# Gated LoRA and low-rank FFN on one core: gh of pairs 1 to 6 transposed by VectorE and by SBUF transfers

## Chip, core and metric

One Trainium2 chip, one core of it. The metric is the device time of the kernel in microseconds (us). Three runs of the kernel before gave 154.99, 155.07 and 155.89 us; the median is 155.07 us.

## What is computed

Cut to what matters, the reference is (x is 2048 x 1024, seen as 32 x 64 rows of 1024; all in float32):

```python
base   = x @ W.T                                   # W 1024 x 1024
logits = x @ Wr.T + 5.0 * one_hot(language_id)     # 8 experts
gates  = softmax over the top 2 logits, 0 for the other experts
h      = x @ A[e].T                                # 8 experts x rank 16
lora   = sum over e, r of h[e, r] * gates[e] * B[e, :, r]
c      = base + 2.0 * lora
out    = x + c @ (U * S @ V.T).T                   # rank 256
```

## The kernel before, in words

The host lays the data out; the kernel never forms base. Since c is only used through V, it first makes P = W.T V (1024 x 256) and BV = 2 B.T V (128 x 256), and then for every row of x: z = x P + gh BV, out = x + z (U S).T, where gh (128 values a row, 8 experts x 16) is h times its gate. All products are float32 split in a high and a low part (x = hi + lo), three matmuls for one: `triple` (L333 to L336) issues hi x hi, lo x hi, hi x lo.

x has 16 tiles of 128 rows. Tiles 2p and 2p+1 are pair p, p from 0 to 7. Names by stage:

- `project(t)` (L379): 8 triples on tile t into bank pj[t % 2], 264 columns: 128 of h, 8 logits, 128 of z (the first half of P's columns). For even t from 2 on, after its fifth triple, `mix(t/2 - 1)` is put in.
- `half_t(p)` (L396): the other half of z, made already transposed (8 triples of 256 columns, both tiles of the pair) in bank zt. After its sixth triple two TensorE transposes (L405) add the first half of z, which ScalarE has copied to z_sb (`copy_z`).
- `transpose_gh(p)` (L413): two TensorE transposes of gh into bank gt (L418). ScalarE casts them to ghT_hi (L624), VectorE subtracts for ghT_lo (L777).
- `mix(p)` (L421): two triples that add gh BV to zt. After it ScalarE and VectorE split zt into hi and lo (`split_za`), and sums of its quarters (`copy_x22`, `sums`, `split_zb`) feed a product of seven terms instead of eight.
- `first_part(p)` (products 1, 6, 7, 5, 2) and `second_part(p)` (products 4, 3), each product one triple of 512 columns into one of four banks fin. VectorE adds them up (`up`) and adds them to x (`xb1`, `xa0`, `xb0`, `xa1`), POOL does three additions more (`sides`, L296).

The order is written out by hand, one instruction list for each engine; semaphores join them. The steady order on PE, for p from 2: project(2p) with mix(p-1), first_part(p-2), project(2p+1), second_part(p-2), half_t(p), transpose_gh(p). VectorE's gates of tile t (`gates_top`, `gates_apply`, ten small operations with the exponential on ScalarE between them) end in gh. SP issues all loads and stores in the steady part: for every p two xt tiles, two x tiles, then the two stores of pair p-2. POOL also makes xT_lo of every tile (L281, 2.4 us), the second one of a pair only when gh of tile 2p+1 is written. Before the pairs stands a stage in which W arrives and P is built; POOL's xT_lo of tile 0 falls into it.

Of the kernel before, what the change touches and what calls it, by code (L numbers as in the profile page):

```python
# [16 lines left out]
def adaln_ffn(nc, xt, x, ids, VW, W, AW, B, U, S, out):  # L17
    P = 128
# [27 lines left out]
    with ExitStack() as ctx:  # L46
# [52 lines left out]
        w_flat = w_raw[:, :, :].rearrange("p c n -> p (c n)")  # L99
        b_raw = w_flat[:, 0:OC * ER].rearrange("p (c n) -> p c n", c=OC)  # L100
# [12 lines left out]
        gt_both = gt[:, 0:2 * P]  # L113
        bv_ps = gt[:, RANK:2 * RANK]
        zt_v = zt[:, :].rearrange("p (m t n) -> p m t n", m=MC, t=2)
# [41 lines left out]
        gt_done = sem("gt_done")  # L157
        gt_hi = sem("gt_hi")
# [22 lines left out]
        LAG = 4  # L181
        PRODS = 7
# [12 lines left out]
        def _(sp):  # L195
# [74 lines left out]
        def _(pool):  # L270
# [12 lines left out]

            def make_tsum(j):
# [20 lines left out]
            split_x(0)  # L305
# [26 lines left out]
        def _(pe):  # L332
# [46 lines left out]
            def project(t):  # L379
# [5 lines left out]
                for k in range(DC):  # L385
# [6 lines left out]
                    if t >= 2 and t % 2 == 0 and k == MH:  # L392
# [3 lines left out]
            def half_t(p):  # L396
                r = (2 * p) % XTR
                dst = zt_v[:, 1, :, :]
                for k in range(DC):
                    last = triple(dst, proj_hi[:, k, TCOLS:COLS], proj_lo[:, k, TCOLS:COLS],  # L400
                                  xT_hi[:, r:r + 2, k, :], xT_lo[:, r:r + 2, k, :], k == 0, False, shared=True)
                    if k == MH + 1:
                        pe.wait_ge(z_copied, 2 * p + 2)
                        for t in range(2):
                            nc.tensor.matmul(zt_v[:, 0, t, :], z_sb[:, t, :], ident[:, :], start=False, stop=False,  # L405
# [7 lines left out]
            def transpose_gh(p):  # L413
                pe.wait_ge(gh_done, 2 * p + 2)
                if p >= 1:
                    pe.wait_ge(gt_lo, p)
                for t in range(2):
                    last = nc.tensor.transpose(gt[:, t * P:(t + 1) * P], gh[:, t, :], ident[:, :])  # L418
                last.then_inc(gt_done, 1)

            def mix(p):  # L421
# [3 lines left out]
                for m in range(MC):  # L425
                    cols = slice(m * P, (m + 1) * P)
                    last = triple(zt[:, 2 * m * P:2 * (m + 1) * P], bv_hi[:, cols], bv_lo[:, cols],
# [94 lines left out]
            for p in range(1, PAIRS):  # L522
# [8 lines left out]
                transpose_gh(p)  # L531
# [24 lines left out]
        def _(act):  # L556
# [41 lines left out]
            def split_za(p):  # L598
                act.wait_ge(zt_done, p + 1)
                zh_free(p)  # L600
                nc.scalar.copy(zh[:, p % 2, 0:MC, :], zt_v[:, :, 0, :]).then_inc(za_hi, 1)

            def split_zb_plain(p):
                act.wait_ge(za_lo, p + 1)
                nc.scalar.copy(zh[:, p % 2, MC:2 * MC, :], zt_v[:, :, 1, :]).then_inc(zb_hi, 1)

            def copy_x22(p):
                if p >= 1:
                    act.wait_ge(zb_lo, p)
                nc.scalar.copy(zs[:, 0, :], zt_v[:, 1, 1, :]).then_inc(x22_copied, 1)  # L610
# [11 lines left out]
            def split_gh(p):  # L622
                act.wait_ge(gt_done, p + 1)
                nc.scalar.copy(ghT_hi[:, :], gt_both).then_inc(gt_hi, 1)  # L624
# [9 lines left out]
            def pair(p):  # L634
                if p < PAIRS - 1:
                    split_x(2 * p + 2)
                split_za(p - 1)
                copy_x22(p - 1)
                copy_u(p - 2)
                copy_z(2 * p)  # L640
                exp_top(2 * p)
                split_zb(p - 1)
                if p < PAIRS - 1:
                    split_x(2 * p + 3)
                copy_z(2 * p + 1)
                exp_top(2 * p + 1)
                split_gh(p)
# [49 lines left out]
            exp_top(3)  # L697
            split_x(5)
            split_gh(1)
# [8 lines left out]
        def _(dve):  # L708
# [66 lines left out]
            def split_gh(p):  # L775
                dve.wait_ge(gt_hi, p + 1)
                nc.vector.tensor_sub(ghT_lo[:, :], gt_both, ghT_hi[:, :].bitcast(F32)).then_inc(gt_lo, 1)  # L777
# [6 lines left out]
            def split_za(p):  # L784
# [3 lines left out]
                nc.vector.tensor_sub(zl[:, p % 2, 0:MC, :], zt_v[:, :, 0, :],  # L788
                                     zh[:, p % 2, 0:MC, :].bitcast(F32)).then_inc(za_lo, 1)

            def split_zb_plain(p):
                dve.wait_ge(zb_hi, p + 1)
                nc.vector.tensor_sub(zl[:, p % 2, MC:2 * MC, :], zt_v[:, :, 1, :],
                                     zh[:, p % 2, MC:2 * MC, :].bitcast(F32)).then_inc(zb_lo, 1)

            def sums(p):
                n = 4 * p
                nc.vector.tensor_add(zs[:, 1, :], zt_v[:, 0, 1, :], zs[:, 0, :]).then_inc(sums_done, 1)
                dve.wait_ge(sums_done, n + 1)
                nc.vector.tensor_sub(zs[:, 2, :], zs[:, 1, :], zt_v[:, 0, 0, :]).then_inc(sums_done, 1)  # L800
                dve.wait_ge(sums_done, n + 2)
                nc.vector.tensor_sub(zs[:, 3, :], zs[:, 0, :], zs[:, 2, :]).then_inc(sums_done, 1)
                nc.vector.tensor_sub(zs[:, 4, :], zt_v[:, 1, 0, :], zs[:, 2, :]).then_inc(sums_done, 1)
# [40 lines left out]

            def pair_2():
# [126 lines left out]
```

## Time and profile before

| | |
|---|---|
| median of three runs | 155.07 us |
| profiled execution, its own time | 155.31 us |
| its span | 153.5 us |
| ScalarE's cast to ghT_hi (L624), mean of 8 | 372 ns |
| ScalarE's cast of zs (L614), mean of 7 | 710 ns |
| ScalarE's copy to z_sb (L628), mean of 16 | 266 ns |
| POOL's addition in `sides` (L296), mean of 21 | 1298 ns |
| load of an xt tile, median from issue to landing | 7.4 us |
| POOL's xT_lo of a tile (L281), mean of 16 | 2404 ns |

The span is that of the profiled execution on the chip; a time in it is read from the span's start. Matmuls overlap: a record lasts longer than the distance to the next one, so what a matmul costs PE is read from the chain of waits, which gives each piece the time until the next one starts. "Idle before" names who released an engine that had stood still.

### The profile page before, as it was taken

Reading aid. Unit: us, or ns where it says so; the run is one execution under the profiler, and the core shown is the slowest. Engines: PE = TensorE matmul, PEld = TensorE weight load, DVE = VectorE, ACT = ScalarE, POOL = GpSimd, SP = SyncE. Lnnn points to the kernel's source line nnn. Section 1 sums busy time; section 2 is a strip of 40 time slices with the busy share of each in tenths; the row PEclk is TensorE's granted clock in tenths of the full one; section 3 lists DMA queues with packets and bytes.
Section 4 is the critical chain, followed back from the end, with each engine's and each line's share of the span. In section 5 each row is a group of like instructions: output and inputs, shape, how many; then the busy total and the mean of one; then the engine's idle time right before and its main releaser. Section 6 shows DMA issues by size and latency. Waiting matters only on the chain.

```text
span 153.5 us, 2910 instructions
## 1 busy us (share of the span) xinstructions
PE 148.2 (97%) x1056; PEld 139.3 (91%) x1056; DVE 106.6 (69%) x297; ACT 63.5 (41%) x141; POOL 71.2 (46%) x56
## 2 busy tenths in 40 slices
PE   7999999999999999899999999999999999999991
PEld 5899989999999988898999899989999998998880
DVE  0776896769578999948674875587559746785951
ACT  3576877884636423346204611361334104013000
POOL 2000233992660666582866196627664640631800
PEclk9999999999999999999999999999999999999999
DMA  5999999999104040069509912990482068006184
GB/s 169 364 386 414 399 409 411 410 406 411 70 4 137 0 137 0 4 255 352 212 19 361 384 62 97 351 367 11 179 265 107 0 260 273 19 0 273 68 334 144
DMA packets 10669, 32.72 MB, mean 213 GB/s; under 512 B 1440, under 2 KB 1952, under 8 KB 10528
## 3 DMA queue, kind: packets, MB, share of 16 engines
q1 hardware_dynamic: 10368, 31.96, 55.4%
q10 hardware_dynamic: 288, 0.59, 1.0%
q8 instruction: 8, 0.13, 0.3%
q14 instruction: 5, 0.04, 0.1%
HBM read 24.16 MB, written 8.39 MB: 212 GB/s over the span
## 4 chain that ended last, share of the span: by engine, by line
PE 80%; DMA 6%; DVE 5%; SPq 4%; issue 2%; DVEq 1%; ACT 0%
PE fin L334 10%; PE pj L335 9%; PE pj L334 9%; PE fin L336 9%; PE fin L335 9%; PE pj L336 9%; PE zt L336 6%; PE zt L334 6%; PE zt L335 6%; DMA xt_raw<-in_xt 6%; SPq L197 2%; DVE w_lo L713 2%; SPq L220 1%; PE gt L418 1%; PE zt L405 1%
## 5 line engine op out<-in xcount | busy, mean ns | idle before, releaser
L281 POOL TENSOR_TENSOR xT_lo<-xt_raw,xT_hi 128x1024 fp32r<-128x1024 f32 x16 | 38.4, 2404 | 40.9 <-ACT xT_hi L582 21.2
L296 POOL TENSOR_TENSOR x_all<-x_all,vw_raw 128x512 f32<-128x512 f32 x21 | 26.6, 1298 | 28.2 <-DVE vw_raw L818 26.3
L334 PE MATMUL pj<-proj_hi,xT_hi 128*128 128x264 f32 x128 | 36.9, 288 | 0.0
L335 PE MATMUL pj<-proj_lo,xT_hi 128*128 128x264 f32 x128 | 36.3, 284 | 0.0
L336 PE MATMUL pj<-proj_hi,xT_lo 128*128 128x264 f32 x128 | 36.2, 283 | 0.0
L334 PE MATMUL fin<-v_hi,w_hi 128*128 128x256 f32 (+1 forms) x88 | 28.1, 320 | 0.2 <-DVE w_lo L713 0.2
L335 PE MATMUL fin<-v_lo,w_hi 128*128 128x256 f32 (+1 forms) x88 | 27.9, 317 | 0.0
L336 PE MATMUL fin<-v_hi,w_lo 128*128 128x256 f32 (+1 forms) x88 | 27.9, 317 | 0.0
L335 PEld LDWEIGHTS pj<-proj_lo,xT_hi 128*128 128x128 f32 x128 | 24.1, 189 | 0.2
L334 PEld LDWEIGHTS pj<-proj_hi,xT_hi 128*128 128x128 f32 x128 | 24.1, 188 | 0.2
L336 PEld LDWEIGHTS pj<-proj_hi,xT_lo 128*128 128x128 f32 x128 | 24.0, 188 | 0.0
L334 PE MATMUL zt<-xT_hi,proj_hi 128*128 128x256 f32 x64 | 18.6, 291 | 0.0
L336 PE MATMUL zt<-xT_hi,proj_lo 128*128 128x256 f32 x64 | 18.0, 281 | 0.0
L335 PE MATMUL zt<-xT_lo,proj_hi 128*128 128x256 f32 x64 | 17.9, 280 | 0.0
L824 DVE TENSOR_TENSOR x_all<-fin,x_all 128x512 f32<-128x512 f32 x28 | 17.9, 682 | 0.0
L334 PEld LDWEIGHTS fin<-v_hi,w_hi 128*128 128x128 f32 x88 | 16.6, 189 | 1.4 <-DVE w_lo L713 0.4
L336 PEld LDWEIGHTS fin<-v_hi,w_lo 128*128 128x128 f32 x88 | 16.6, 189 | 1.2
L335 PEld LDWEIGHTS fin<-v_lo,w_hi 128*128 128x128 f32 x88 | 16.6, 189 | 0.8
L582 ACT CAST xT_hi<-xt_raw 128x1024 fp32r<-128x1024 f32 x16 | 16.8, 1049 | 1.0 <-DMA xt_raw<-in_xt 1.0
L628 ACT COPY z_sb<-pj 128x128 f32<-128x128 f32 x16 | 4.3, 266 | 22.8 <-DVE logit L745 22.8
L334 PE MATMUL fin<-us_hi,w_hi 128*128 128x512 f32 (+1 forms) x31 | 11.9, 383 | 0.8 <-DVE x_all L824 0.8
L335 PEld LDWEIGHTS zt<-xT_lo,proj_hi 128*128 128x128 f32 x64 | 12.0, 188 | 0.3
(93 smaller groups left out, 272.6 us busy)
## 6 DMA issues: line engine op xcount, KB each, us to landing
xt_raw<-in_xt SPq DMA_DIRECT2D x16, 512.0 KB, 7.4
x_all<-in_x SPq DMA_DIRECT2D x16, 512.0 KB, 6.5
out<-x_all SPq DMA_DIRECT2D x13, 512.0 KB, 3.1
vw_raw<-in_VW SPq DMA_DIRECT2D x6, 384.0 KB, 8.0
w_raw<-in_W SPq DMA_DIRECT2D x8, 256.0 KB, 7.4
out<-x_all SPq DMA_DIRECT2D x5, 256.0 KB, 2.0
w_raw<-in_U SPq DMA_DIRECT2D x1, 1024.0 KB, 6.9
aw_raw<-in_AW SPq DMA_DIRECT2D x1, 544.0 KB, 8.1
```

Of the source, the lines that this page charges most:

```text
L197: sp.dma_start(w_raw[:, k, :], W[k, :, :]).then_inc(w_load[k], 16)
L220: sp.dma_start(vw_raw[:, k, :], VW[k, :, :]).then_inc(vw_load[k], 16)
L281: nc.gpsimd.tensor_sub(xT_lo[:, t % XTR, :, :], xt_raw[:, t % XTR, :, :], xT_hi[:, t % XTR, :, :].bitcast(F32)).then_inc(xt_lo, 1)
L296: nc.gpsimd.tensor_add(x_all[:, t % XR, cols], x_all[:, t % XR, cols], ups[:, j, :]).then_inc(side_add, 1)
L334: nc.tensor.matmul(dst, l_hi, r_hi, start=first, stop=False, skip_group_check=shared)
L335: nc.tensor.matmul(dst, l_hi, r_lo, start=False, stop=False, skip_group_check=shared)
L336: return nc.tensor.matmul(dst, l_lo, r_hi, start=False, stop=last, skip_group_check=shared)
L405: nc.tensor.matmul(zt_v[:, 0, t, :], z_sb[:, t, :], ident[:, :], start=False, stop=False, is_transpose=True, skip_group_check=True)
L582: nc.scalar.copy(xT_hi[:, t % XTR, :, :], xt_raw[:, t % XTR, :, :]).then_inc(xt_hi, 1)
L628: nc.scalar.copy(z_sb[:, t % 2, :], pj[t % 2][:, Z0:TCOLS]).then_inc(z_copied, 1)
L713: nc.vector.tensor_sub(w_lo[:, i % WRING, :], w_chunk(i), w_hi[:, i % WRING, :].bitcast(F32)).then_inc(w_lo_done, 1)
L824: nc.vector.tensor_add(x_all[:, t % XR, cols], src[:, :], x_all[:, t % XR, cols]).then_inc(fin_read, 1)
```

## The change

VectorE turns gh of pairs 1 to 6 in 32 x 32 blocks from gh into `blk`, each block in its own place (`turn_gh`). The blocks off the diagonal then have to change places: SP issues twelve SBUF-to-SBUF transfers of 32 partitions x 2 tiles x 32 columns from `blk` to `tr` (`move_blocks`), and ScalarE copies the four diagonal blocks (`move_diagonal`). `blk` and `tr` lie in the unused part of w_raw and have two slots each. ScalarE and VectorE make ghT_hi and ghT_lo from `tr` (`split_gh_moved`). Pairs 0 and 7 keep the TensorE transposes; that of pair 7 writes into pj[0].

With it go these moves. mix(p-1) for pairs from 1 on stands in project(2p+1), not in project(2p). zt alternates between two banks, zt and gt, and `zt_free` waits for the pair before the last. VectorE's and ScalarE's order inside a pair is changed, and xT_lo of tile 0 is made in two halves.

```diff
+        blk = w_flat[:, 8 * P:12 * P].rearrange("p (q m n) -> p q m n", q=2, m=2)
+        tr = w_flat[:, 16 * P:20 * P].rearrange("p (q m n) -> p q m n", q=2, m=2)
...
-        zt_v = zt[:, :].rearrange("p (m t n) -> p m t n", m=MC, t=2)
+        zt_bank = [zt, gt]
+        zt_v = [b[:, :].rearrange("p (m t n) -> p m t n", m=MC, t=2) for b in zt_bank]
...
+            def move_blocks(p):
+                sp.wait_ge(blk_done, p)
+                for i in range(SQS):
+                    for j in range(SQS):
+                        if i != j:
+                            sp.dma_start(tr[SQ * j:SQ * (j + 1), p % 2, :, SQ * i:SQ * (i + 1)],
+                                         blk[SQ * i:SQ * (i + 1), p % 2, :, SQ * j:SQ * (j + 1)]).then_inc(tr_load, 16)
...
                     load_x(2 * p + 1)
+                if p < PAIRS - 1:
+                    move_blocks(p)
                 if p >= 2:
                     store_pair(p - 2)
...
-            split_x(0)
+            split_x_half(0, 0)
+            split_x_half(0, 1)
...
-                    if t >= 2 and t % 2 == 0 and k == MH:
+                    if t == 2 and k == MH:
+                        mix(0)
+                    if t >= 5 and t % 2 == 1 and k == MH:
                         mix(t // 2 - 1)
...
             def zt_free(p):
-                pe.wait_ge(za_lo, p)
-                pe.wait_ge(sums_done, 4 * p)
+                if p == 1:
+                    pe.wait_ge(bv_lo_done, 1)
+                if p >= 2:
+                    pe.wait_ge(za_lo, p - 1)
+                    pe.wait_ge(sums_done, 4 * (p - 1))
...
                 half_t(p)
-                transpose_gh(p)
+            transpose_gh(PAIRS - 1)
...
+            def split_gh_moved(p):
+                act.wait_ge(tr_load, MOVES * p)
+                act.wait_ge(tr_diag, SQS * p)
+                nc.scalar.copy(ghT_hi[:, :], tr[:, p % 2, :, :]).then_inc(gt_hi, 1)
+
+            def move_diagonal(p):
+                act.wait_ge(blk_done, p)
+                for i in range(SQS):
+                    rows = slice(SQ * i, SQ * (i + 1))
+                    nc.scalar.copy(tr[rows, p % 2, :, rows], blk[rows, p % 2, :, rows]).then_inc(tr_diag, 1)
...
             def pair(p):
                 if p < PAIRS - 1:
                     split_x(2 * p + 2)
+                copy_u(p - 2)
+                if p == 2:
+                    split_gh_moved(1)
+                copy_z(2 * p)
+                exp_top(2 * p)
+                if p < PAIRS - 1:
+                    split_x(2 * p + 3)
+                if p >= 3:
+                    split_gh_moved(p - 1)
                 split_za(p - 1)
                 copy_x22(p - 1)
-                copy_u(p - 2)
-                copy_z(2 * p)
-                exp_top(2 * p)
                 split_zb(p - 1)
-                if p < PAIRS - 1:
-                    split_x(2 * p + 3)
                 copy_z(2 * p + 1)
                 exp_top(2 * p + 1)
-                split_gh(p)
+                if p < PAIRS - 1:
+                    move_diagonal(p)
+                else:
+                    split_gh(p)
...
+            def turn_gh(p):
+                dve.wait_ge(gh_done, 2 * p + 2)
+                nc.vector.transpose(blk[:, p % 2, :, :], gh[:, :, :]).then_inc(blk_done, 1)
...
             def pair(p):
-                split_zb(p - 2)
-                split_za(p - 1)
-                sums(p - 1)
-                gates_top(2 * p)
-                gates_apply(2 * p)
-                up(p - 2, 1)
-                up(p - 2, 2)
-                xb1(p - 2)
-                xa0(p - 2)
-                gates_top(2 * p + 1)
-                gates_apply(2 * p + 1)
-                xb0(p - 2)
-                xa1(p - 2)
-                if p == PAIRS - 1:
-                    split_zb(p - 1)
-                split_gh(p)
+                gates(2 * p)
+                up(p - 2, 1)
+                up(p - 2, 2)
+                split_gh_moved(p - 1)
+                xb1(p - 2)
+                xa0(p - 2)
+                split_za(p - 1)
+                sums(p - 1)
+                gates(2 * p + 1)
+                if p < PAIRS - 1:
+                    turn_gh(p)
+                    xb0(p - 2)
+                    xa1(p - 2)
+                    split_zb(p - 1)
+                else:
...
+                    split_gh(p)
```

VectorE, pair 4, from the end of its first gates on, before (w_lo is zl and vw_raw is ups, which lie in those tiles; the rows of the second gates are left out):

```order
L770 SCALAR_TENSOR_TENSOR gh<-pj,rsum,gate 128x128
L818 TENSOR_TENSOR vw_raw<-fin,vw_raw 128x512 x2
L824 TENSOR_TENSOR x_all<-fin,x_all 128x512 x2
L745 SCALAR_TENSOR_TENSOR logit<-target,pj 128x8
...
L770 SCALAR_TENSOR_TENSOR gh<-pj,rsum,gate 128x128
L824 TENSOR_TENSOR x_all<-fin,x_all 128x512 x2
L777 TENSOR_TENSOR ghT_lo<-gt,ghT_hi 128x256
L807 TENSOR_TENSOR w_lo<-zs,w_hi 128x640
L788 TENSOR_TENSOR w_lo<-zt,w_hi 128x256
```

The same place with the change (w_raw holds blk and tr):

```order
L819 SCALAR_TENSOR_TENSOR gh<-pj,rsum,gate 128x128
L877 TENSOR_TENSOR vw_raw<-fin,vw_raw 128x512 x2
L831 TENSOR_TENSOR ghT_lo<-w_raw,ghT_hi 128x256
L883 TENSOR_TENSOR x_all<-fin,x_all 128x512 x2
L847 TENSOR_TENSOR w_lo<-gt,w_hi 128x256
L857 TENSOR_TENSOR zs<-gt,zs 128x128
L859 TENSOR_TENSOR zs<-zs,gt 128x128
...
L819 SCALAR_TENSOR_TENSOR gh<-pj,rsum,gate 128x128
L836 STREAM_TRANSPOSE w_raw<-gh 128x256
L883 TENSOR_TENSOR x_all<-fin,x_all 128x512 x2
L866 TENSOR_TENSOR w_lo<-zs,w_hi 128x640
```

ghT_lo now reads `tr` in SBUF and stands between `up` and xb1; the splits of zt (w_lo, zs) come before the second gates, and the block transpose right behind them.

SP with the change, pair 3 (w_raw<-w_raw are the twelve transfers):

```order
L210 DMA xt_raw<-in_xt 128x1024 x2
L215 DMA x_all<-in_x 128x1024 x2
L255 DMA w_raw<-w_raw 32x2x32 x12
L219 DMA out<-x_all 128x1024
L221 DMA out<-x_all 128x1024
```

Twelve issues stand between the loads of a pair and the stores of the pair before the last; before, nothing stood there.

## Rows read from the trace of the kernel before

**Rows 1.** The page: busy us, share of the span, instructions.
```profile
PE 148.2 (97%) x1056; PEld 139.3 (91%) x1056; DVE 106.6 (69%) x297; ACT 63.5 (41%) x141; POOL 71.2 (46%) x56
```

**Rows 2.** Windows: length, busy of PE, PEld, DVE, ACT, POOL, clock, DMA, GB/s.
```profile
50.50:66.20 15.70, 14.86 (x106) 13.66 (x105) 14.02 (x35) 5.24 (x13) 10.28 (x6) 1.00 0.11 34
95.37:109.95 14.58, 14.58 (x105) 13.73 (x105) 9.70 (x33) 5.05 (x13) 8.60 (x6) 1.00 0.59 217
```

**Rows 3.** Chain of waits, pair 5: start us, us, what.
```profile
95.37 0.12 PE pj L334
...
97.18 0.12 PE zt L334
...
98.98 0.23 PE fin L334
...
102.39 0.12 PE pj L334
...
105.29 0.23 PE fin L334
...
106.67 0.12 PE zt L334
...
108.80 0.22 PE zt L405 x2
...
109.73 0.22 PE gt L418 x2
```

**Rows 4.** Timeline of PE, pair 2: start us, us, instruction, idle before.
```profile
60.73 0.39 PE L336 MATMUL fin<-v_hi,w_lo 128*128 128x512 f32 x1
61.95 0.50 PE L334 MATMUL fin<-us_hi,w_hi 128*128 128x512 f32 x1 [0.84 <-DVE x_all L824]
```

**Rows 5.** Timeline while P is built: PE, POOL, VectorE.
```profile
20.81 0.28 PE L336 MATMUL fin<-v_hi,w_lo 128*128 128x256 f32 x1
21.32 0.38 PE L334 MATMUL fin<-v_hi,w_hi 128*128 128x256 f32 x1 [0.22 <-DVE w_lo L713]
...
18.31 2.39 POOL L281 TENSOR_TENSOR xT_lo<-xt_raw,xT_hi 128x1024 fp32r<-128x1024 f32 x1 [16.43 <-ACT xT_hi L582]
...
18.78 2.48 DVE L713 TENSOR_TENSOR w_lo<-w_raw,w_hi 128x512 fp32r<-128x512 f32 x1 [0.59 <-ACT w_hi L567]
```

**Rows 6.** Timeline of SP: issues.
```profile
3.08 0.43 SPq L223 DMA_DIRECT2D ids_i<-in_ids  x1
3.56 0.43 SPq L220 DMA_DIRECT2D vw_raw<-in_VW  x1
...
66.57 2.02 SPq L202 DMA_DIRECT2D xt_raw<-in_xt  x2
```

**Rows 7.** The page, DMA issues: count, KB, median us from issue to landing.
```profile
out<-x_all SPq DMA_DIRECT2D x2, 128.0 KB, 1.9
```

**Rows 8.** Groups by form: busy us, mean ns, idle before.
```profile
L777 DVE TENSOR_TENSOR ghT_lo<-gt,ghT_hi 128x256 fp32r<-128x256 f32 x8 | 3.4, 424 | 10.3 <-ACT ghT_hi L624 10.3
...
L713 DVE TENSOR_TENSOR w_lo<-vw_raw,w_hi 128x512 fp32r<-128x512 f32 x8 | 5.5, 687 | 0.2
```

**Rows 9.** Timeline of VectorE, pair 5.
```profile
99.95 0.15 DVE L745 SCALAR_TENSOR_TENSOR logit<-target,pj 128x8 f32<-128x8 f32 x1
...
101.53 0.35 DVE L770 SCALAR_TENSOR_TENSOR gh<-pj,rsum,gate 128x128 f32<-128x128 f32 x1
101.79 1.51 DVE L818 TENSOR_TENSOR vw_raw<-fin,vw_raw 128x512 f32<-128x512 f32 x2
```

**Rows 10.** Timeline, pair 2: POOL, then VectorE.
```profile
57.50 2.59 POOL L296 TENSOR_TENSOR x_all<-x_all,vw_raw 128x512 f32<-128x512 f32 x2
...
57.31 0.29 DVE L800 TENSOR_TENSOR zs<-zs,zt 128x128 f32<-128x128 f32 x1
57.63 1.30 DVE L802 TENSOR_TENSOR zs<-zs 128x128 f32<-128x128 f32 x1
```

**Rows 11.** The page, DMA queue: packets, MB, share of 16 engines.
```profile
q1 hardware_dynamic: 10368, 31.96, 55.4%
```

More of the change, by code:

```diff
@@ L181, in adaln_ffn @@
         LAG = 4
+        SQ = 32
+        SQS = P // SQ
+        MOVES = 16 * SQS * (SQS - 1)
         PRODS = 7
@@ L282, in split_x, with split_x_half @@
                                      xT_hi[:, t % XTR, :, :].bitcast(F32)).then_inc(xt_lo, 1)
+            def split_x_half(t, h):
+                pool.wait_ge(xt_hi, t + 1)
+                ks = slice(h * MH, (h + 1) * MH)
+                op = nc.gpsimd.tensor_sub(xT_lo[:, t % XTR, ks, :], xt_raw[:, t % XTR, ks, :],
+                                          xT_hi[:, t % XTR, ks, :].bitcast(F32))
+                if h == 1:
+                    op.then_inc(xt_lo, 1)
             def make_tsum(j):
@@ L404, in half_t @@
                         for t in range(2):
-                            nc.tensor.matmul(zt_v[:, 0, t, :], z_sb[:, t, :], ident[:, :], start=False, stop=False,
+                            nc.tensor.matmul(zt_v[p % 2][:, 0, t, :], z_sb[:, t, :], ident[:, :], start=False, stop=False,
                                              is_transpose=True, skip_group_check=True)
@@ L609, in copy_x22 @@
                     act.wait_ge(zb_lo, p)
[L610 removed]
+                nc.scalar.copy(zs[:, 0, :], zt_v[p % 2][:, 1, 1, :]).then_inc(x22_copied, 1)
             def split_zb(p):
@@ L843, in residual_end, with gates @@
                 nc.vector.tensor_add(x_all[:, t % XR, lo:hi], src[:, 0:hi - lo], x_all[:, t % XR, lo:hi]).then_inc(end_read, 1)
+            def gates(t):
+                gates_top(t)
+                gates_apply(t)
             def pair_2():
@@ L847, in pair_2 @@
                 split_us(1)
[L848 removed]
                 up(0, 1)
                 up(0, 2)
+                split_gh_moved(1)
+                xb1(0)
+                gates(4)
+                split_za(1)
                 sums(1)
[L852 to L854 removed]
+                gates(5)
+                turn_gh(2)
                 xa0(0)
[L856 to L857 removed]
                 xb0(0)
                 xa1(0)
[L860 removed]
+                split_zb(1)
             def pair(p):
[L863 removed]
+                gates(2 * p)
[4 more added lines that the diff above has]
+                xa0(p - 2)
                 split_za(p - 1)
                 sums(p - 1)
[L866 to L878 removed]
+                gates(2 * p + 1)
[3 more added lines that the diff above has]
+                    xa1(p - 2)
+                    split_zb(p - 1)
+                else:
+                    split_zb(p - 1)
+                    xb0(p - 2)
+                    xa1(p - 2)
+                    split_gh(p)
             dve.wait_ge(vw_load[0], 16)
@@ L909, in _ @@
             sums(0)
-            gates_top(2)
-            gates_apply(2)
-            gates_top(3)
-            gates_apply(3)
+            gates(2)
+            gates(3)
+            turn_gh(1)
             split_t(1)
-            split_gh(1)
             pair_2()
```

47 lines of the change are left out of this document (23 added, 24 removed).

## The prediction

> **What bounds the kernel now.** I read the busy shares first: TensorE is busy 97% of the span, VectorE 69% [rows 1]. By stretch it is tighter: from the pair that starts at 95.37 us to the next, 14.58 us are 14.58 us of PE; only the pair from 50.50 to 66.20 is longer, 15.70 us with 14.86 busy [rows 2]. The granted clock is 1.00, the 2.4 GHz level, throughout. The chain of waits, read next, is an unbroken row of matmuls in a middle pair, so it gives the schedule of PE [rows 3]. Count from T, the start of project(2p) (95.37): the mix of pair p-1 at T+1.8, first_part at T+3.6, project(2p+1) at T+7.0, second_part at T+9.9, half_t at T+11.3, z's two transposes at T+13.4, gh's two at T+14.36, next pair at T+14.58. So a PE instruction that goes is worth its time there, as long as no other engine comes late. The whole question is whether any does.
>
> **The removed transposes.** The chain gives a pair's two transposes of gh as 0.22 us [rows 3]; the 272 ns of a single record is latency, since the next matmul starts before it ends. Six pairs lose them: 6 x 0.22 = -1.32 us. Pairs 0 and 7 keep theirs. The Trainium skill ("VectorE: DVE Perf Modes", The three transpose paths) gives 390 ns for a 128x128 transpose on TensorE and 311 ns on VectorE, and its rules for authors send a 128x128 transpose to TensorE. By its figure the removal would be an estimate of 6 x 0.78 = -4.7 us; this trace shows 0.22 us for two, and that decides.
>
> **The first tile's split in two halves.** At 18.31 POOL starts xT_lo of tile 0 (2.39 us). VectorE's w_lo at 18.78 has two SBUF inputs and takes 2.48 us, where its sisters take 0.69 [rows 8]: it stands still until POOL is done, and PE starts its next matmul at 21.32 where 20.93 was due by the 0.12 us rhythm [rows 5]. With halves VectorE waits for 1.2 us less, which covers the whole hole: -0.38 us. (Bounds: 0 if the second half gets in ahead of VectorE, -0.4.)
>
> **The new path of gh.** The mix now stands in project(2p+1), so call its start M = T + 7.0 + 5 x 0.36 minus the 0.70 us of mix that leaves project(2p) = T+8.1. The pair is 14.36 us by PE alone. What follows M in today's order: logit starts 2.77 us behind the mix's start (99.95 against 97.18), gh is written at 101.88, so M+4.7 [rows 3, 9]; ScalarE's cast of zs now stands before the exponential of the odd tile and adds some 0.2: gh at M+4.9. Then, none of it in the trace of before:
> - VectorE's block transpose, 128x256. Nearest row: the subtraction of the same size, 0.42 us [rows 8]. I take 0.42; below, half of it; above, twice.
> - Twelve transfers on SP. The issue of 8 KB of ids and the one after it start 0.48 us apart, and both take 0.43, so size is not what counts; with the ring full two took 2.02 us [rows 6]. I take 0.48, because the queue is idle then: the last starts 11 x 0.48 = 5.3 us after the first. Ends: 0.3 us, if fewer rows (32 for 128) make it cheaper, and 1.0 us.
> - Its landing: 1.9 us, as the smallest stores had [rows 7].
> - ScalarE's four diagonal copies (some 0.8 us) lie beside the transfers and cost nothing; without that cover they would be 0.8 us.
> - ScalarE's cast 0.37 us and VectorE's subtraction 0.42 us, as before [rows 8].
>
> Sum with 0.1 us at each hand-over: landed at M + 4.9 + 0.5 + 0.1 + 5.3 + 1.9 = M+12.7, ready for the mix at M+13.6. PE wants it at M+14.36. So the transfers are hidden with 0.75 us to spare, and PE does not wait in a middle pair. The same in T: landed at T+6.4, when VectorE has done gates(2p) and both up adds (about T+6.9).
>
> **A new collision.** ghT_lo was PSUM minus SBUF; of a moved gh it reads two SBUF tiles. Such an operation of VectorE stands still beside POOL: zs at 57.63 took 1.30 us, the zs before it 0.29, up to the end of POOL's first addition; POOL's three additions (1.3 us each) start when up(p-2,1) is done, T+6.2, just ahead of it. In a middle pair VectorE gets in when the first ends, at T+7.5, and is done at T+7.8: 0.3 us to spare. Nothing there, but the cover is thin.
>
> **What queues behind.** On SP the stores of pair p-3 and the loads of xt now come after the twelve issues, 5.6 us later; the xt they bring is cast some 8 us after its issue and lands 7.4 us after it in the median, so it just arrives: nothing. On VectorE the residual adds xb0 and xa1 stand behind the block transpose, 0.42 us; bank_c and bank_d are needed only at T+4.3 of the next pair. Nothing. On POOL the split of tile 2p+3 starts with gh as before.
>
> **Pair 2.** Today PE stands from 60.96 to 61.95 = 0.99 us behind the late VectorE work of this pair [rows 4]. In the new order that add (xb1) is early, but z's copy is late: moves of pair 1 land at about 57.4, ghT_lo is done at 58.2, then xb1 0.7, gates(4) 1.9 plus up to 1.3 behind POOL's additions, za 0.4, sums 1.1, the cast of zs 0.7, copy 0.3: z is there at 63.3 to 64.6, and PE is at z's transposes at 63.7. So the old wait goes and one of 0 to 0.9 comes: -0.99 to 0. I take 0, since dtop and chosen (two SBUF inputs) both fall into POOL's three additions. **Pair 3** then inherits it: gates(5) ends 1.5 us later than in a middle pair, POOL's splits shift with it, the first dtop waits for one of them (2.4 us), up comes at T+7, and ghT_lo runs into the additions and is ready at T+9.2 instead of T+8.1: 0 to +1.2, I take +1.1. After that the middle-pair schedule holds.
>
> **Sum.** -1.32 - 0.38 + 0 + 1.1 = -0.6 us on the profiled execution's 155.31 us (span 153.5): 154.7; it is 0.24 above the median 155.07, so 154.5 us.
>
> **Rivals.**
> 1. *The thin places hold.* No wait in pair 3 and pair 2 between its bounds: -1.7 to -2.7, that is 153.4 to 152.4 us. For it: each collision of pairs 2 and 3 hangs on who starts first within 0.1 us. Against: POOL is busy for most of that pair.
> 2. *The moves come late, slower.* If they land more than 0.75 us later (the transfers' pitch at 0.55 us is enough, or a transpose of 0.84 with a landing of 2.3), ScalarE's cast is done after POOL's second addition has begun, and ghT_lo waits for its end: about +1.1 us in each of five pairs (mixes 2 to 6), one of which the forecast has: 154.5 + 4.4 = 158.9 us. It gets worse if packets, not issues, set the pace: the packets of the main queue took 55.4% of 16 engines x 153.5 us, 131 ns each [rows 11]; a move is 64 packets, four and a closing one on each engine, 0.66 us at that price, 7.9 us for twelve. Ready at M+16.2, the pair would be 16.2 us, +1.8 each: about 163 us. Against: these packets hold 128 B, those 3 KB. The Trainium skill ("DMA: Bandwidth & Descriptors", Measured under Bandwidth) says that transfers under 64 KB are descriptor-dominated and gives 0.68 us for a 4 KB one of 64 packets; by it twelve in a row are an estimate of 8.2 us, and that speaks against the change. No row of before has packets so small, alone.
> 3. *split_zb loses its place.* Behind the residual adds it has two SBUF inputs and meets POOL's split of tile 2p+3, until T+1.2 of the next pair. If POOL then starts tile 2p+4 ahead of it, zb is ready at T+4.4, and PE wants it at T+3.6: +0.8 us in each of three or four pairs, 157 us. For it: POOL's next input is cast at just that time. Against: VectorE has then been waiting, and a waiting VectorE got in between two additions at 58.8 [rows 10].
>
> **Numbers.** Forecast 0.36; rival 1 0.31; rival 2 0.22; rival 3 0.11. I take 1% (1.55 us) as what can be told from no change. Faster by over 1% (under 153.52) is rival 1 and the forecast's edge: 0.33. Slower by over 1% (above 156.62): rival 2 and half of rival 3, 0.27. Within: 0.40. Forecast's own range 153.5 to 155.5. For 8 in 10 the range goes from 152.4, the best sum, to 159.3, past the first step of rival 2; the packet-bound part of it and little else is left out.
>
> **What would show it.** Right: middle pairs of 14.36 us, all PE; SP's twelve issues 0.48 us apart; the last landing at T+6.4; a PE wait before z's transposes in pair 2 and before the mix in project(7). PE waits on ghT_lo in every pair speak for rival 2, on w_lo<-zs for rival 3. A pitch far below 0.4 us or a move landing in under 1.5 us would leave more slack than I give it; a shift of POOL's additions by half a microsecond would change pairs 2 and 3 and make the sum wrong by up to 2 us.

## The result and the profile after

The changed kernel takes 165.95 us (median of 6 runs, 164.61 to 166.85) beside 155.22 us for the kernel before on the same chip: ratio 1.068, 95% interval 1.063 to 1.073. The forecast was 154.5 us in a range of 152.4 to 159.3, so the time lies above all of it. The mechanism that happened is rival 2, the moves that come late; it was given 0.22.

The profiled execution took 164.61 us with a span of 162.8, so 9.3 us more than the 155.31 and 153.5 of before. The page after, busy shares first (they answer [rows 1]), then the queue ([rows 11]), the chain that ended last, and the transfers among the DMA issues:

```profile
PE 148.1 (91%) x1044; PEld 138.3 (85%) x1044; DVE 112.1 (69%) x303; ACT 69.0 (42%) x165; POOL 73.5 (45%) x57
...
q1 hardware_dynamic: 16128, 32.56, 54.6%
...
PE 36%; SPq 25%; DVE 14%; DMA 10%; ACT 8%; issue 4%; DVEq 2%
SPq L255 25%; DMA w_raw<-w_raw 7%; PE fin L361 7%; PE fin L363 7%; PE fin L362 7%; DMA w_raw<-in_W 3%; ACT w_hi L645 2%; PE gt L361 2%; PE pj L361 2%; PE pj L362 2%; PE pj L363 2%; DVE w_raw L836 2%; PE zt L361 2%; DVEq L796 2%; PE gt L363 2%
...
w_raw<-w_raw SPq DMA_DIRECT2D x72, 8.0 KB, 1.8
```

PE is as busy as before in microseconds, and its share of the span is six points lower. A quarter of the critical chain is one line, L255: not the data of the transfers but SP's work of issuing them.

The mixes of the six moved pairs start at 60.29, 77.75, 94.15, 110.15, 126.35 and 141.94 us, so they are 17.5, 16.4, 16.0, 16.2 and 15.6 us apart. Windows of about one such distance each (columns as in [rows 2]; the second is exactly from mix to mix):

```profile
78.50:94.15 15.65, 13.88 (x98) 12.82 (x97) 10.21 (x34) 5.94 (x17) 8.79 (x5) 1.00 0.56 199
94.15:110.15 16.00, 14.63 (x102) 13.57 (x102) 10.98 (x35) 5.94 (x17) 8.93 (x5) 1.00 0.56 196
110.15:126.00 15.85, 14.62 (x101) 13.57 (x101) 10.63 (x34) 5.94 (x17) 8.91 (x5) 1.00 0.58 206
126.00:142.00 16.00, 14.68 (x102) 13.63 (x102) 11.22 (x36) 4.05 (x15) 6.20 (x4) 1.00 0.43 145
```

A pair that took 14.58 us now takes some 16 us, and PE stands in each. What it stands for, PE's waits (us in total, times, longest):

```profile
PE gt L361 <- DVE ghT_lo L831: 5.4, 3, 2.1
PE zt L361 <- DVE ghT_lo L831: 4.3, 3, 2.0
...
PE zt L434 <- ACT z_sb L670: 0.6, 1, 0.6
```

All six mixes of moved pairs wait for ghT_lo, 9.7 us in all. A first matmul behind such a wait takes 0.39 us in the chain where one in a row takes 0.12, 6 x 0.27 = 1.6 more. With 0.6 for z_sb, less the 0.99 of [rows 4] and the 1.32 of the transposes, that is 9.6, against the 9.3 between the two profiled executions.

The chain of waits through one such pair (start us, us, what) shows what holds ghT_lo up:

```profile
94.15 0.39 PE gt L361
...
95.16 0.37 ACT w_hi L632
...
98.90 0.36 DVE gh L819
99.28 0.46 DVE w_raw L836
99.75 0.59 SPq L255
100.39 0.60 SPq L255
...
106.14 1.23 SPq L255
107.42 1.79 DMA w_raw<-w_raw
109.23 0.41 ACT ghT_hi L660
109.67 0.43 DVE ghT_lo L831
110.15 0.39 PE zt L361
```

It is a closed loop of 16.0 us. The mix at 94.15 releases the split of zt; behind that on VectorE and ScalarE come the gates; gh is written at 99.26, turned, moved by twelve issues one behind the other, cast, and only then may the next mix start, at 110.15. PE needs 14.36 us for a pair, so it waits for the loop each time.

The chain names eleven issues; the twelfth starts at 107.42, and the 1.79 us of the DMA piece run from there, from the start of that issue, to the landing. SP's own timeline gives this set and the next (start, us, what):

```profile
99.75 8.26 SPq L255 DMA_DIRECT2D w_raw<-w_raw  x12
115.75 7.63 SPq L255 DMA_DIRECT2D w_raw<-w_raw  x12
```

An issue takes 0.60 us and the next one starts 0.64 us after it. Eleven such steps are 7.0 us; in the set at 99.75 the eleventh issue took 1.23 us, so that the last starts 7.7 us after the first.

### The profile page after: what moved, and what is told of

Read it like the earlier page. It is cut to its first block, busy times and chain, and to the rows that moved or that the text cites. A ratio compares the mean times of both kernels' runs of the same rounds, so it can differ in the third digit from the quotient of the medians.

```text
span 162.8 us, 2987 instructions
## 1 busy us (share of the span) xinstructions
PE 148.1 (91%) x1044; PEld 138.3 (85%) x1044; DVE 112.1 (69%) x303; ACT 69.0 (42%) x165; POOL 73.5 (45%) x57
## 4 chain that ended last, share of the span: by engine, by line
PE 36%; SPq 25%; DVE 14%; DMA 10%; ACT 8%; issue 4%; DVEq 2%
SPq L255 25%; DMA w_raw<-w_raw 7%; PE fin L361 7%; PE fin L363 7%; PE fin L362 7%; DMA w_raw<-in_W 3%; ACT w_hi L645 2%; PE gt L361 2%; PE pj L361 2%; PE pj L362 2%; PE pj L363 2%; DVE w_raw L836 2%; PE zt L361 2%; DVEq L796 2%; PE gt L363 2%
## 5 line engine op out<-in xcount | busy, mean ns | idle before, releaser
L299 POOL TENSOR_TENSOR xT_lo<-xt_raw,xT_hi 128x1024 fp32r<-128x1024 f32 x15 | 37.7, 2522 | 32.6 <-DVE gh L819 18.4
L361 PE MATMUL pj<-proj_hi,xT_hi 128*128 128x264 f32 x128 | 36.4, 284 | 0.0
L831 DVE TENSOR_TENSOR ghT_lo<-w_raw,ghT_hi 128x256 fp32r<-128x256 f32 x6 | 3.2, 538 | 13.6 <-ACT ghT_hi L660 13.6
L363 PE MATMUL fin<-us_hi,w_lo 128*128 128x512 f32 (+1 forms) x31 | 11.7, 377 | 0.0
L362 PE MATMUL fin<-us_lo,w_hi 128*128 128x512 f32 (+1 forms) x31 | 11.7, 376 | 0.0
L877 DVE TENSOR_TENSOR vw_raw<-fin,vw_raw 128x512 f32<-128x512 f32 x14 | 9.6, 687 | 3.0 <-PE fin L363 2.2
L660 ACT CAST ghT_hi<-w_raw 128x256 fp32r<-128x256 f32 x6 | 2.4, 405 | 20.3 <-DMA w_raw<-w_raw 20.3
```

The lines of the kernel that those rows point to most:

```text
L299: nc.gpsimd.tensor_sub(xT_lo[:, t % XTR, :, :], xt_raw[:, t % XTR, :, :], xT_hi[:, t % XTR, :, :].bitcast(F32)).then_inc(xt_lo, 1)
L361: nc.tensor.matmul(dst, l_hi, r_hi, start=first, stop=False, skip_group_check=shared)
L362: nc.tensor.matmul(dst, l_hi, r_lo, start=False, stop=False, skip_group_check=shared)
L363: return nc.tensor.matmul(dst, l_lo, r_hi, start=False, stop=last, skip_group_check=shared)
L877: nc.vector.tensor_add(ups[:, j, :], (bank_b if j == 1 else bank_c)[:, :], ups[:, j - 1, :]).then_inc(fin_read, 1)
```

## Experiments

Times are medians; a ratio is to the kernel before on the same chip, with its 95% interval. The kernel before took 155.11 to 155.22 us beside these experiments, so times of different experiments can be compared to about 0.1 us as far as the chip goes.

### no_moves: the transfers left out

```diff
-                for i in range(SQS):
-                    for j in range(SQS):
-                        if i != j:
-                            sp.dma_start(tr[...], blk[...]).then_inc(tr_load, 16)
...
-                act.wait_ge(tr_load, MOVES * p)
```

> The changed kernel without its 72 transfers: the blocks off the diagonal never change places, so gh of pairs 1 to 6 is wrong; all else is as in the change. Theory A (the issues on SP close a loop from mix to mix that is longer than PE's work): in the change a middle pair is 16.00 us (94.15 to 110.15); without the transfers nothing that is issued stands between the block transpose and the casts, the loop is shorter than PE's 14.36 us and the pair is 14.36. Pairs 3 to 7 give back 5 x 1.6 = 8 us and pair 2 its wait of 2.1: 165.9 - 10 to 12 = 154 to 156 us. Theory B (the new order, the second zt bank or the collisions of VectorE with POOL are what costs): the time stays above 160 us and PE goes on waiting for ghT_lo.

Measured: 154.81 us (154.53 to 155.45), ratio 0.998 (0.997 to 1.000). Everything else of the change, the new order, the block transposes and the diagonal copies, is in this kernel, so the 72 transfers and the wait for them cost 11.1 us in this order (9.8 between the two profiled executions, 164.61 and 154.78). PE's waits in it (timeline, idle before in brackets):

```profile
64.32 0.44 PE L429 MATMUL zt<-ident,z_sb 128*128 128x128 f32 x2 [0.88 <-ACT z_sb L664]
74.25 0.39 PE L356 MATMUL zt<-ghT_hi,bv_hi 128*128 128x256 f32 x1 [0.65 <-DVE ghT_lo L825]
```

These are the two waits that the forecast named, before z's transposes in pair 2 and before the mix in project(7). What it forecast is close to the kernel that one gets when the moves are in time: 154.81 for 154.5. Two errors partly cancel in that: the -0.38 of the first tile's halves did not come (halves_only below), and the wait in project(7) costs 0.65 and the 0.27 of a late first matmul, where 1.1 was entered.

### ten_moves: two transfers fewer in each pair

```diff
-        MOVES = 16 * SQS * (SQS - 1)
+        MOVES = 16 * (SQS * (SQS - 1) - 2)
...
-                        if i != j:
+                        if i != j and (i, j) not in ((0, 1), (1, 0)):
```

> The change with ten transfers a pair instead of twelve (blocks (0,1) and (1,0) are left where they were, so that part of gh is wrong). Theory A, the number of issues times their pitch: two issues of 0.64 us fewer are 1.28 us off every loop, 16.0 to 14.7, still above 14.36. Five loops and the first one: 165.9 - 6 x 1.28 = 158.2 us. Rival A2, the latency of the last landing or a queue that has to drain counts and not the number: under 2 us of gain, 164 to 165 us. Rival B (order and collisions): no change, 165.9 us.

Measured: 157.25 us (156.76 to 157.44), ratio 1.013 (1.011 to 1.015); 8.7 us off for twelve issues in all (7.2 between the profiled executions). Its sets on SP (start, us, count):

```profile
96.15 6.35 SPq L255 DMA_DIRECT2D w_raw<-w_raw  x10
111.67 6.36 SPq L255 DMA_DIRECT2D w_raw<-w_raw  x10
```

Ten take 6.35 us, 0.64 each. From the first set to the sixth it is 75.7 us (50.35 to 126.05), in the change 82.0 (49.93 to 131.95): 1.26 us less a pair in the mean, two issues at 0.64. That is the slope of a loop, one to one, but only in the mean: the five distances are 18.1, 15.4, 16.4, 16.0 and 16.2 us in the change and 16.2, 14.1, 15.5, 15.5 and 14.4 here. Two of the latter are down at PE's own 14.36, and a long issue or a late landing falls into other sets than in the change. PE still waits 3.3 us for ghT_lo, 0.9 at the longest.

### rows256: the same bytes as 32 rows of 256 B, without a third dimension

```diff
-        blk = w_flat[:, 8 * P:12 * P].rearrange("p (q m n) -> p q m n", q=2, m=2)
+        blk = w_flat[:, 8 * P:12 * P].rearrange("p (q j m n) -> p q j m n", q=2, j=4, m=2)
...
-                            sp.dma_start(tr[SQ * j:SQ * (j + 1), p % 2, :, SQ * i:SQ * (i + 1)],
-                                         blk[SQ * i:SQ * (i + 1), p % 2, :, SQ * j:SQ * (j + 1)]).then_inc(tr_load, 16)
+                            sp.dma_start(tr[SQ * j:SQ * (j + 1), p % 2, i, :, :].rearrange("p m n -> p (m n)"),
+                                         blk[SQ * i:SQ * (i + 1), p % 2, j, :, :].rearrange("p m n -> p (m n)")).then_inc(tr_load, 16)
```

The block transpose, the diagonal copies, the cast and the subtraction follow this layout (not shown).

> The same twelve transfers a pair and the same result, with blk and tr laid out so that the 32 columns of both tiles lie side by side: a transfer has 32 rows of 256 bytes instead of 64 of 128. In the change an issue takes 0.60 us, against 0.43 for a full-width load. If the number of rows or the third dimension of the pattern makes the issue dearer (theory A3), it falls to 0.43 and the pitch from 0.64 to 0.48: 11 x 0.16 = 1.8 us off each loop, the middle pair at 14.4, and the whole at 155.5 to 157.5 us. If the issue costs 0.60 because both ends are in SBUF or for another reason that has nothing to do with rows, the time stays at 165 to 166.

Measured: 165.53 us (164.78 to 167.47; without the highest of the four, 165.16), ratio 1.071 (1.064 to 1.078). The issues of the change first, then those of this kernel (ns, least/median/most):

```profile
L255 SPq DMA_DIRECT2D w_raw<-w_raw x72: 586/597/1233, 49.9 to 139.0; - x72
```

```profile
L255 SPq DMA_DIRECT2D w_raw<-w_raw x72: 507/591/1267, 49.7 to 138.6; - x72
```

Half the rows, the same issue, and no gain that can be told from the change. By the queue's count a transfer is 48 packets here (13824 in all, less the 10368 of [rows 11], over 72) and 80 in the change. Neither the packets nor this change of shape set the pace.

### issue_forms: what does the 0.60 us hang on?

Each pair's twelve transfers in another form, to spare columns; order and number as before. One execution, 161.63 us. Its whole time is not the point.

```diff
+                            if p == 1:
+                                sp.dma_start(two[b, :, :], blk[a, d, :, b])...    # 32 x 2 x 128 B, SBUF to SBUF
+                            elif p == 2:
+                                sp.dma_start(flat[b, :], x_v[0, a, 0:64])...      # 32 x 256 B, HBM to SBUF
+                            elif p == 3:
+                                sp.dma_start(two[:, :, :], blk[:, d, :, b])...    # 128 x 2 x 128 B, SBUF to SBUF
+                            elif p == 4:
+                                sp.dma_start(flat[b, :], blk[a, d, 0, 0:64])...   # 32 x 256 B, SBUF to SBUF
+                            elif p == 5:
+                                sp.dma_start(flat[:, :], x_v[0, :, 0:64])...      # 128 x 256 B, HBM to SBUF
+                            elif p == 6:
+                                sp.dma_start(flat[:, :], blk[:, d, 0, 0:64])...   # 128 x 256 B, SBUF to SBUF
```

> Not a time but a measurement of SP's issues: the twelve transfers of every moved pair go to a spare place, in another form for each pair (the exchanged blocks never reach tr, so gh is wrong). Pair 1: as in the change, 32 rows x 2 x 128 B, SBUF to SBUF. Pair 2: 32 rows of 256 B from HBM. Pair 3: 128 rows x 2 x 128 B, SBUF to SBUF. Pair 4: 32 rows of 256 B, SBUF to SBUF. Pair 5: 128 rows of 256 B from HBM. Pair 6: 128 rows of 256 B, SBUF to SBUF. If 0.60 us is the price of both ends in SBUF, pairs 2 and 5 show 0.43 and the others 0.60. If it is the price of 32 rows, pairs 3, 5 and 6 show 0.43. If it is the price of a transfer behind others still in flight, all six show 0.6.

Measured (ns, least/median/most, and when the first and the last started), in the order of the six forms:

```profile
L261 SPq DMA_DIRECT2D w_raw<-w_raw x12: 596/597/756, 49.8 to 57.0; - x12
L263 SPq DMA_DIRECT2D w_raw<-in_x x12: 340/421/427, 67.8 to 72.8; - x12
L265 SPq DMA_DIRECT2D w_raw<-w_raw x12: 593/622/1189, 81.8 to 90.2; - x12
L267 SPq DMA_DIRECT2D w_raw<-w_raw x12: 590/591/1181, 98.7 to 106.2; - x12
L269 SPq DMA_DIRECT2D w_raw<-in_x x12: 328/432/437, 114.6 to 119.7; - x12
L271 SPq DMA_DIRECT2D w_raw<-w_raw x12: 527/601/604, 129.0 to 136.0; - x12
```

All four forms with both ends in SBUF take 0.59 to 0.62 us in the median, with 32 rows or 128, in two dimensions or three. Both forms from HBM take 0.42 to 0.43, one behind the other as well. So of what was varied here the issue's price goes by where the ends lie; larger transfers and other destinations were not in this run. The 0.43 of [rows 6] was the price of a load from HBM.

### split_queue: four of the twelve issued by ScalarE

```diff
+        ACT_MOVES = ((3, 2), (3, 1), (3, 0), (2, 3))
...
-                        if i != j:
+                        if i != j and (i, j) not in ACT_MOVES:
...
             def move_diagonal(p):
                 act.wait_ge(blk_done, p)
+                for i, j in ACT_MOVES:
+                    act.dma_start(tr[...], blk[...]).then_inc(tr_load, 16)
```

> The change with eight of the twelve transfers issued by SP and four by ScalarE, ahead of its diagonal copies. Theory A: SP's last issue starts 7 x 0.64 = 4.5 us after its first, not 7.0 or more; ScalarE's four are out before. That is 2.6 us off a loop of 16.0: PE's 14.36 again, unless ScalarE's 2.4 us of issuing delay its copy of u and with it ghT_lo by up to 1 us. 155 to 158 us. Rival: the two queues share what makes an issue slow, so that twelve issues take as long from two engines as from one: 164 to 168 us.

Measured: 165.22 us (163.72 to 165.44), ratio 1.065 (1.064 to 1.067). A miss for the theory: the time lies in the range of its rival, but not for the rival's reason. SP's eight issues do get through sooner, the last one 5.4 us after the first in the pair shown (one took 1.10 us) and 4.5 in three other sets, which is seven steps of 0.64, although ScalarE issues at the same time. ScalarE, then VectorE, in a middle pair (timelines, idle before in brackets):

```profile
100.28 2.83 ACTq L666 DMA_DIRECT2D w_raw<-w_raw  x4
103.15 1.04 ACT L670 COPY w_raw<-w_raw 32x64 f32<-32x64 f32 x4 [4.24 <-issue]
104.22 1.05 ACT L614 CAST xT_hi<-xt_raw 128x1024 fp32r<-128x1024 f32 x1
...
105.81 0.21 ACT L678 ACTIVATE etop<-dtop 128x2 f32<-128x2 f32 x1
...
107.46 0.41 ACT L661 CAST ghT_hi<-w_raw 128x256 fp32r<-128x256 f32 x1 [0.41 <-DMA w_raw<-w_raw]
```

```profile
106.15 0.16 DVE L815 RECIPROCAL rsum<-esum 128x1 f32<-128x1 f32 x1 [0.91 <-ACT etop L678]
106.23 1.56 DVE L817 TENSOR_TENSOR pick<-chosen,etop 128x16 f32<-128x16 f32 x1
...
108.29 1.50 DVE L881 TENSOR_TENSOR vw_raw<-fin,vw_raw 128x512 f32<-128x512 f32 x2
109.71 0.89 DVE L835 TENSOR_TENSOR ghT_lo<-w_raw,ghT_hi 128x256 fp32r<-128x256 f32 x1
```

The moves did land earlier: ghT_hi is cast 8.0 us behind the start of gh (99.42 to 107.46); in the change it was 10.3 (98.90 to 109.23). But the four issues hold ScalarE for 2.8 us, its exponential comes late, VectorE waits 0.91 for it, then meets POOL's split (pick takes 1.56 us for 0.16), and ghT_lo is done at 110.6; the pair is 16.0 us again (mixes at 94.65 and 110.65). The delay went from SP to ScalarE and VectorE. Why it comes to just 16.0 again is not shown.

### pe_all: the new order, with gh transposed by TensorE in all pairs

```diff
-            transpose_gh(PAIRS - 1)
+                transpose_gh(p)
...
-        zt_bank = [zt, gt]
+        zt_bank = [zt, zt]
```

turn_gh, move_blocks and move_diagonal are gone, and split_gh reads gt in every pair; since gt is taken by gh, zt has one bank.

> The order of the change (mix in project(2p+1), VectorE's and ScalarE's new order, the first tile in halves) with TensorE transposing gh in all eight pairs, as before, into gt; zt in one bank. No block transpose, no transfer. If the order costs nothing but what no_moves shows, this is no_moves plus six pairs of transposes: 154.8 + 6 x 0.22 = 156.1 us, perhaps 0.5 more if half_t has to wait for the one zt bank (the splits end 0.3 us ahead of it). If the order alone were harmful without anything late in it: above 157.5. If the order is a gain by itself: below 155.1.

Measured: 156.08 us (155.70 to 157.04), ratio 1.007 (1.004 to 1.009). The new order brings nothing by itself; it costs 0.9 us, with a wait of 1.4 us of PE for the sums of zt, which stands in the way of the single bank. Beside no_moves it is 1.27 us slower, where 6 x 0.22 = 1.32 was priced. Their waits differ too (1.4 here, 0.9 and 0.7 there), so this bears the price of the transposes out without being a clean measurement of it.

### halves_only: the kernel before with tile 0's split in two halves

```diff
-            split_x(0)
+            split_x_half(0, 0)
+            split_x_half(0, 1)
```

> The kernel before with POOL's xT_lo of tile 0 in two halves and nothing else. The prediction's term: VectorE's w_lo, 2.48 us long behind POOL, ends 1.2 us earlier, and the hole of 0.38 us on PE before its matmul at 21.32 goes: 154.7 us. Rival: the second half gets in ahead of VectorE's next operation with two SBUF inputs, v_lo, and the hole only moves: 155.1 us, 0 to -0.15.

Measured: 155.19 us beside 155.22, ratio 1.000 (0.998 to 1.002). POOL, then VectorE while P is built (timelines, for [rows 5]):

```profile
17.91 2.99 POOL L287 TENSOR_TENSOR xT_lo<-xt_raw,xT_hi 128x512 fp32r<-128x512 f32 x2 [16.02 <-ACT xT_hi L591]
```

```profile
18.40 1.34 DVE L722 TENSOR_TENSOR w_lo<-w_raw,w_hi 128x512 fp32r<-128x512 f32 x1 [0.54 <-ACT w_hi L576]
19.67 1.51 DVE L727 TENSOR_TENSOR v_lo<-vw_raw,v_hi 128x256 fp32r<-128x256 f32 x1
21.10 0.68 DVE L722 TENSOR_TENSOR w_lo<-vw_raw,w_hi 128x512 fp32r<-128x512 f32 x1
```

w_lo gets through in 1.34 us instead of 2.48, but POOL's second half comes ahead of VectorE's next subtraction, which takes 1.51 us for 0.42. The wait was handed on.

### late_mix: the mix taken out of the loop

The 72 transfers stay. mix(p-1) goes from project(2p+1) to behind second_part(p-2); VectorE makes gates(2p+1) and the block transpose ahead of the split of zt, so that gh no longer follows the mix.

```diff
-                    if t >= 5 and t % 2 == 1 and k == MH:
-                        mix(t // 2 - 1)
...
                     second_part(p - 2)
+                    mix(p - 1)
...
-                split_gh_moved(p - 1)
                 xb1(p - 2)
                 xa0(p - 2)
-                split_za(p - 1)
-                sums(p - 1)
+                split_gh_moved(p - 1)
                 gates(2 * p + 1)
                 if p < PAIRS - 1:
                     turn_gh(p)
+                split_za(p - 1)
+                sums(p - 1)
```

ScalarE's order is changed in the same way (not shown): copy_z and the exponential of tile 2p+1 and the diagonal copies come ahead of its casts of zt.

> The change with the same 72 transfers, but mix(p-1) behind second_part(p-2) instead of inside project(2p+1), and the gates of tile 2p+1 and the block transpose ahead of the splits of zt on VectorE and ScalarE. Theory A says the transfers cost because they lie on a loop: mix -> splits of zt -> gates -> transpose -> 12 issues -> casts -> next mix, 16.0 us. Here gh of tile 2p+1 no longer waits for the mix, so there is no loop: gh is there at T+11.3, the moves have landed at about T+21, and the mix that wants them stands at T+25. PE never waits in a middle pair: 14.36 us a pair and 152.5 to 154.0 us in all, below the kernel before. Rival: the transfers cost by themselves (SP's 8 us a pair delay loads or stores, or the collisions with POOL grow with the new order): 157 us or more.

Measured: 158.09 us (157.85 to 158.21), ratio 1.018 (1.017 to 1.020). 7.9 us come back with every transfer still there. But the number missed its range and lies in that of the rival (157 or more), so this run alone does not decide; late_mix2 and late_no_moves below do. PE's waits:

```profile
PE gt L361 <- DVE ghT_lo L827: 2.0, 1, 2.0
PE fin L361 <- DVE w_lo L862: 1.2, 4, 0.3
...
PE gt L361 <- DVE ghT_lo L822: 0.6, 1, 0.6
```

No middle mix waits for ghT_lo any more. What is left are places of this order: in pair 2 ghT_lo(1) stood behind gates(4), whose small operations are stretched beside POOL's additions, and a residual add; at the end ghT_lo(7) stood behind two residual adds; and in four middle pairs the split of the sums was late, because on ScalarE the diagonal copies stood ahead of the cast of zt (timeline):

```profile
80.03 1.04 ACT L665 COPY w_raw<-w_raw 32x64 f32<-32x64 f32 x4 [1.37 <-DVE w_raw L832]
81.10 0.37 ACT L631 CAST w_hi<-zt 128x256 fp32r<-128x256 f32 x1
```

### late_mix2 and late_no_moves: those three places mended, with and without the transfers

```diff
-                if p < PAIRS - 1:
-                    move_diagonal(p)
                 split_za(p - 1)
                 copy_x22(p - 1)
+                if p < PAIRS - 1:
+                    move_diagonal(p)
                 split_zb(p - 1)
...
-                gates(4)
-                xa0(0)
-                split_gh_moved(1)
+                gates_top(4)
+                split_gh_moved(1)
+                gates_apply(4)
+                xa0(0)
...
                     split_zb(p - 1)
+                    split_gh(p)
                     xb0(p - 2)
                     xa1(p - 2)
-                    split_gh(p)
```

late_no_moves takes the lines of no_moves out of it.

> late_mix with three moves in the order: on ScalarE split_za(p-1) and copy_x22(p-1) stand ahead of the diagonal copies; on VectorE ghT_lo(1) stands between gates_top(4) and gates_apply(4); at the end ghT_lo(7) stands ahead of xb0(6) and xa1(6). Nothing is left out. Theory A (once the mix stands outside of the loop, the transfers cost nothing, and what late_mix lost was these three places): 158.1 minus four waits of about 0.6 for the product of the sums, minus 1.95 in pair 2, minus 0.57 at the end, so 153.2, between 152.5 and 154; no wait of PE for ghT_lo over 0.2 us in pairs 3 to 6. Rival (the waits only move: VectorE stretched beside POOL's additions stays late in each pair): 155.5 or more, with PE waiting for w_lo or ghT_lo elsewhere in the middle pairs, loop above 14.7 us.

> late_mix2 without the 72 transfers and without the wait for them; what it leaves out is the off-diagonal blocks of gh of pairs 1 to 6. Theory A (twelve issues of 0.60 us and their landing lie fully beside other work in this order): within 0.4 us of late_mix2. Rival (the transfers still set something, by ghT_hi that waits for the last landing or by stores that SP issues later): 1 us or more below late_mix2.

Measured: late_mix2 154.42 us (154.08 to 154.75), ratio 0.994 (0.992 to 0.997); late_no_moves 154.27 us (154.04 to 154.61), ratio 0.993 (0.991 to 0.995). Their difference is 0.15 us, less than the intervals can tell. In this order 72 transfers cost next to nothing, in the change's order 11.1 us; so the loop is shown, and that the transfers cost by themselves is ruled out. Yet SP works as long as before (timeline of late_mix2):

```profile
93.43 8.48 SPq L255 DMA_DIRECT2D w_raw<-w_raw  x12
101.95 0.58 SPq L219 DMA_DIRECT2D out<-x_all  x1
...
107.52 7.63 SPq L255 DMA_DIRECT2D w_raw<-w_raw  x12
```

From the first set to the sixth it is 72.1 us (50.20 to 122.32), 14.4 a pair. The one wait left in the pairs is a new one, in pair 2 (PE's waits of late_mix2):

```profile
PE fin L361 <- DVE w_lo L862: 1.3, 1, 1.3
```

VectorE is behind there: ghT_lo(1) takes 0.92 us and one of the sums 1.28 beside POOL, and two residual adds stand ahead of the split of the sums. late_no_moves has the same wait, 1.2 us, so it comes from the order and not from the transfers. Without it 154.42 would be 153.1, where 153.2 was expected; that it would come was not in the expectation. late_mix2 leaves nothing out and is 0.6% (0.75 us) under the kernel before. How much of that is owed to the transposes and how much to the order is not shown: no run has this order with TensorE's transposes in all pairs.

## Why the prediction was wrong

Step by step, with the words of the prediction's parts:

- **The removed transposes, -1.32.** As far as the runs tell, right: 1.27 us between pe_all and no_moves. The other price, -4.7 us by the Trainium skill's 390 ns ("VectorE: DVE Perf Modes", The three transpose paths; its figure is for bf16, these are float32), is far from it.
- **The first tile's split, -0.38.** Wrong: 0. The text had this case as a bound ("if the second half gets in ahead of VectorE") and took the other.
- **The new path of gh: the step that failed.** From the mix to the next one's operands:

| us from M | predicted | chain after |
|---|---|---|
| gh written | 4.9 | 5.1 |
| first issue starts | 5.5 | 5.6 |
| start of the first issue to start of the last | 5.3 | 7.7 |
| landing, from the start of the last issue | 1.9 | 1.8 |
| casts and hand-overs | 0.9 | 0.9 |
| mix may start | 13.6 | 16.0 |

The step that failed is one factor of one term: the 0.48 us from one issue to the next, times eleven. It was 0.64, so the twelve issues took 11 x 0.16 = 1.8 us more, in every set. The remaining 0.6 us of the 2.4 is the one issue of 1.23 us in this set. With 1.8 alone the mix could start at 13.6 + 1.8 = M+15.4, still 1.0 us after PE wants it, and in a loop that is lost in every pair. The last distance between mixes, in which no issue and no landing was late, is 15.6 us. The other parts of this path, the landing among them, were within 0.2 us. The 0.48 came from loads out of HBM, whose issue is 0.43; with both ends in SBUF it is 0.60, and in issue_forms rows and dimensions hardly moved that (medians of 591 to 622 ns). The prediction said "size is not what counts", which holds for the forms tried, and set ends of 0.3 and 1.0 us; the value taken was the wrong one between them, and 0.55 was known to be enough to tip it. It named a full ring for the 2.02 us of two loads in [rows 6]; no row shows one. Nor is it known why single issues were long (1.23 and 0.94 us in two sets of the change, 0.60 in nearly all) and why the last landing of two sets took 2.1 and 2.6 us instead of 1.8; they are what takes the pair from some 15.4 to 16 us. (The first distance, 17.5 us, has neither; there gh is written only 7.2 us after the mix, at 67.48.)
- **Rival 2.** The mechanism and the place are right, with PE waits on ghT_lo in every pair as its sign. Its first price, +1.1 in five pairs for 158.9 us, was too small: it was the wait for one more addition of POOL, for moves that only just miss the slack. Its second (pair 16.2 us, 163 us) comes close to the pair of 16.0 by a wrong cause, so by luck: packets. The Trainium skill's 0.68 us for a small transfer of 64 packets ("DMA: Bandwidth & Descriptors", Measured under Bandwidth; measured there from HBM to SBUF and issued by GpSimd) lies near the pitch of 0.64 too, but if each packet had its price, rows256 with 48 for 80 should have been quicker. It was not, and ten_moves follows the number of issues. The sum also lacked the sixth mix and the 0.27 us that a matmul behind a wait takes more. The upper end 159.3 was cut just where that rival's dearer half began.
- **A new collision, pair 2, pair 3.** In the change the one of pair 2 shows as 0.6 us for z_sb, and the other cannot be told apart from the wait for the loop. In no_moves both show: 0.88 us before z's transposes (0 to 0.9, the upper end taken), 0.65 before the mix in project(7) (+1.1 taken). Rival 1 did not happen there.
- **Rival 3.** Not in the change. PE never waits for the sums there, because the pair is longer. In late_mix2 a wait for the same operation behind the residual adds appears, 1.3 us in pair 2.
- **What queues behind on SP.** Nothing, as predicted: no cast of xt waits in the change for more than 0.5 us, though the loads come behind some 8 us of issues.

## What to carry over

When a path is replaced by a row of small transfers, price it by the issuing queue: the distance from one issue to the next, times the count less one, plus the landing as it is counted from the start of an issue; and take the distance from a row with the same endpoints. Ask then whether the path lies in a loop of the program: in a loop an overshoot is paid in every round (two issues a pair were 1.26 us a pair in the mean), outside of it the same 8 us of SP cost 0.15 us in all. And a large range of an unknown (here 0.3 to 1.0 us, times twelve) belongs into the range of the time, not only into a rival.

## Of the hardware, not expected

- An issue on SP takes 0.60 us (pitch 0.64) with both ends in SBUF and 0.43 (pitch 0.46 to 0.48) from HBM, with 32 or 128 rows. ScalarE's queue has a like price: four in 2.83 us, beside SP's.
- VectorE's 32x32 block transpose of 128x256 float32 takes 0.45 us, about as long as a subtraction of that size (0.42).
- Six runs of the change show a mean granted clock between 0.969 and 0.998, and the time rises as it falls (164.61 us at 0.998, 165.51 at 0.990, 166.07 at 0.979, 166.85 at 0.969); the kernel before stands at 1.00 [rows 2]. Of a pair's 16.0 us PE stands some 1.4, which before it did not. Whether that is why the clock falls at times was not tried; between these runs it goes with 2.2 us. In late_mix it goes with nothing: 157.85 and 158.03 us at 0.988, 158.15 and 158.21 at 1.00.
